# Two-layer adaLN transformer: how the first attention is started up (first head's keys in pieces, its queries placed by matmuls, modulation rows spread over lead chunks)

## The chip, the cores and the metric

One core of one Trainium2 chip. The time is the device time of one execution in microseconds (us). Engines: TensorE (PE; its weight loads PEld), VectorE (DVE), ScalarE (ACT), GpSimd (POOL), and SyncE (SP), which issues the DMAs.

## The reference

Two layers over x of 1024 tokens x 256. Each layer computes six modulation vectors from a condition vector c and then an attention and an expert part:

```
mod = silu(c) @ wmod            -> sa, ca, ga, sb, cb, gb   (256 each)
ga, gb = sign * max(|.|, 0.25)
h = layernorm(x) * (1 + ca) + sa;  x = x + ga * attention(h)
h = layernorm(x) * (1 + cb) + sb;  x = x + gb * experts(h)
```

Attention of layer 0: Q = h @ Wq.T, 16 heads of 16, against 4096 given keys and values per head, softmax, times Wo. Layer 1 has its own projections over the 1024 tokens. The change concerns the start: the modulation vectors of both layers, the first layernorm and projection, and the first head's keys and queries.

## The kernel before, in words

All engines run their own list of instructions; semaphores order them. The order on each engine is written out by hand, so an engine stands still at a wait even where later work is ready.

`Front.register` (lines 966 to 1082) is the start. SP issues the loads in this order: c, x in two halves, the wmod columns of sa and ca of layer 0, the identity, head 0's keys (`load_k`, six loads of 128 KB: three copies into each of two strips of 64 partitions), wq, head 0's values; when the keys have landed, the rest of wmod of layer 0 and all of layer 1. TensorE runs 90 filler matmuls (`keep_busy`, line 1179), the column products of sa and ca (line 1086: one-column matmuls that leave the vector along partitions), 20 fillers, and 16 transposes of the normalised x. ScalarE scales and shifts these into h_t (line 1076).

`Projection` makes Q in four pieces of 128 channels x 512 tokens (line 1282). Each is split into a high part (ScalarE, fp32r, line 1314) and a low part, the rest (VectorE, line 1329), so that a product of parts keeps the precision. Pieces 0 and 1 hold heads 0 to 7. Rows of one head go by DMA (`send_rows`, line 73) into `q_rows`: per strip 48 partitions, high, low, high, against keys high, high, low. GpSimd splits the keys in the same way (`split_keys`: high part of all 128 partitions, line 423; two low parts of 16 partitions, line 428).

`Attention.run` goes over 32 half heads u (512 queries each). First pass, for the row maxima: 16 chunks per half head, each 128 queries x 2 x 512 keys (line 646, two matmuls into one of two bank pairs), reduced by VectorE (line 820). GpSimd splits the maxima in four small steps (line 571 and on), TensorE turns them (line 668), ScalarE puts them beside the queries. Second pass: 32 chunks of scores per half head (line 710), exp by ScalarE (line 912), values (line 689). The first pass runs 22 chunks ahead: 22 lead chunks stand before the first chunk of the second pass.

The later modulation vectors are computed in that lead: two row products (line 1093: c broadcast to 128 columns as weights, 256 columns of wmod moving, so each partition gets the whole row) after 45 fillers before chunk 0, then a group behind each chunk from 2 on, alternately column and row groups, with three fillers ahead of a column group and none ahead of a row; `groups` lists them. All results are taken at once by ScalarE (`take_later`) when the last is there. mod_col holds vectors along partitions, mod_row along the free axis.

The loop that issues the lead chunks:

```
for n in range(ahead):
    first_wait(n)
    if n >= 2: keep_busy(pe, psum, self.ident_bf, filling, 2 * (n % 2))
    first_half(n, 0)
    first_half(n, 1).then_inc(self.s1_full, 1)
    front.later_products(pe, n)
```

## Time and profile before

| | us |
|---|---|
| median of 3 runs | 1781.34 (1774.15 to 1800.0) |
| profiled execution | 1779.75, its span 1777.9 |
| TensorE busy in the span | 1703.0 (96%) |
| VectorE, ScalarE, GpSimd busy | 1388.6, 1149.9, 518.6 |
| mean granted TensorE clock | 0.987 |

Busy time of TensorE counts a matmul that is slow because of a low clock at its slow duration. A row of the timeline merges like instructions that follow each other; x4 is their count. The bracket is the idle time of that engine before it and what ended it. PEclk is the granted clock as a share of full speed.

### The profile page before, as it was taken

What the parts mean: (1) busy time and instruction counts of PE and PEld (TensorE: products, weight loads), DVE (VectorE), ACT (ScalarE), POOL (GpSimd) and SP (SyncE); (2) the same over time, 40 slices, a digit from 0 to 9 for tenths busy, and PEclk for the clock granted to TensorE, in tenths of its full rate; (3) what the DMA queues carried; (4) which work ended last, traced back from release to release, by engine and by line L of the source; (5) the groups of instructions that cost most, each with busy time, mean ns of one, the idle gap of its engine ahead of it and who ended that gap; (6) DMA issues with size and microseconds to landing.
All of it is one profiled execution on the core that took longest, in us unless ns stands there. A gap on an engine that the chain in (4) does not pass through costs nothing. (4 is left out here: it accounts for less than half of the span.)

```text
span 1777.9 us, 33654 instructions
## 1 busy us (share of the span) xinstructions
PE 1703.0 (96%) x12560; PEld 1045.4 (59%) x12563; DVE 1388.6 (78%) x1927; ACT 1149.9 (65%) x2277; POOL 518.6 (29%) x535
## 2 busy tenths in 40 slices
PE   8999999999999999889999989999999999789998
PEld 6433333333333333565444468888888888668886
DVE  4899999999999997367999667677767777746665
ACT  2588888888888888465888545454545454533333
POOL 7446334333344522002334301110211020142221
PEclk8999999999999999989999999999999999989999
DMA  7123322223322300103446210000000000024332
GB/s 177 30 46 65 55 50 45 46 57 75 70 46 57 71 26 11 37 19 57 123 114 165 69 32 16 9 24 15 24 9 24 15 12 0 19 86 115 110 103 77
DMA packets 50305, 97.88 MB, mean 55 GB/s; under 512 B 11481, under 2 KB 21817, under 8 KB 48651
## 3 DMA queue, kind: packets, MB, share of 16 engines
q1 hardware_dynamic: 49899, 95.78, 22.8%
q8 instruction: 78, 1.28, 0.3%
q10 hardware_dynamic: 288, 0.49, 0.2%
q14 instruction: 40, 0.33, 0.1%
HBM read 64.58 MB, written 15.92 MB: 45 GB/s over the span
## 5 line engine op out<-in xcount | busy, mean ns | idle before, releaser
L912 ACT ACTIVATE a_probs<-psum 128x512 f32<-128x512 f32 x1280 | 693.2, 597 | 121.6 <-PE psum L710 91.5
L820 DVE TENSOR_REDUCE a_max_part<-psum 128x1 f32<-128x1024 f32 x512 | 621.8, 1223 | 44.7 <-PE psum L646 42.8
L710 PE MATMUL psum<-a_q_max,a_k_rows 51*128 51x512 f32 x1280 | 409.2, 465 | 0.8 <-ACT a_probs L912 0.7
L689 PE MATMUL psum<-a_probs,a_v_ext 128*32 128x256 f32 (+1 forms) x4600 | 395.1, 415 | 7.3 <-issue 7.2
L646 PE MATMUL psum<-a_k_rows,a_q_rows 48*128 48x512 f32 x1280 | 355.4, 430 | 0.0
L710 PEld LDWEIGHTS psum<-a_q_max,a_k_rows 51*128 51x128 f32 x1280 | 167.0, 184 | 270.1 <-ACT a_probs L912 215.5
L689 PEld LDWEIGHTS psum<-a_probs,a_v_ext 128*32 128x32 f32 x4600 | 91.3, 107 | 206.7 <-issue 105.6
L646 PEld LDWEIGHTS psum<-a_k_rows,a_q_rows 48*128 48x128 f32 x1280 | 152.7, 187 | 9.3 <-issue 3.1
L2228 PE MATMUL psum<-high_t_parts,high_gu 128*128 128x512 f32 x600 | 148.9, 398 | 9.1 <-POOL high_gu L2346 7.5
L816 DVE TENSOR_REDUCE a_neg_max<-psum 128x1 f32<-128x1024 f32 x128 | 150.7, 1219 | 8.2 <-PE psum L646 8.0
L428 POOL TENSOR_TENSOR a_k_rows<-a_k_in,a_k_rows 16x2048 fp32r<-16x2048 f32 x32 | 146.0, 4562 | 2.5
L571 POOL TENSOR_TENSOR a_max_bf<-a_neg_max,a_zeros 128x8 bf16<-128x8 f32 x64 | 14.7, 230 | 443.1 <-issue 392.2
L2228 PEld LDWEIGHTS psum<-high_t_parts,high_gu 128*128 128x128 f32 x600 | 114.0, 191 | 36.6 <-POOL high_gu L2346 8.2
L1792 PE MATMUL psum<-wide_k_t,wide_q_t 128*128 128x512 f32 (+3 forms) x576 | 130.6, 353 | 1.5 <-DVE wide_k_t L1990 1.5
L1792 PE MATMUL psum<-wide_p_t,wide_v 128*128 128x512 f32 (+3 forms) x576 | 109.6, 344 | 5.1 <-DVE x L2001 5.1
L1792 PEld LDWEIGHTS psum<-wide_p_t,wide_v 128*128 128x128 f32 x576 | 97.6, 188 | 22.3 <-issue 6.3
L1933 ACT ACTIVATE wide_probs<-psum,wide_neg_max 128x128 f32<-128x128 f32 (+7 forms) x128 | 96.5, 754 | 21.6 <-DVE wide_neg_max L2023 21.6
L2012 DVE TENSOR_TENSOR wide_p_t<-psum,wide_p_t 128x512 fp32r<-128x512 f32 (+1 forms) x192 | 100.0, 548 | 12.4 <-ACT wide_p_t L1918 12.4
L1792 PE MATMUL psum<-wide_t_parts,wide_wqk 128*128 128x512 f32 x384 | 102.2, 401 | 6.2 <-DVE wide_v L1990 3.9
L1918 ACT ACTIVATE wide_p_t<-psum 128x512 fp32r<-128x512 f32 (+1 forms) x192 | 87.1, 493 | 28.0 <-PE psum L1833 28.0
L1792 PEld LDWEIGHTS psum<-wide_k_t,wide_q_t 128*128 128x128 f32 x576 | 94.0, 188 | 12.6 <-issue 1.9
L2023 DVE TENSOR_REDUCE wide_neg_max<-psum 128x1 f32<-128x128 f32 (+7 forms) x128 | 97.0, 758 | 4.4
(263 smaller groups left out, 2143.2 us busy)
## 6 DMA issues: line engine op xcount, KB each, us to landing
o<-a_o_out SPq DMA_DIRECT2D x56, 256.0 KB, 2.3
a_k_in<-in_k SPq DMA_DIRECT2D x96, 128.0 KB, 4.6
a_q_rows<-q_high SPq DMA_DIRECT2D x124, 64.0 KB, 2.4
gu_in<-in_w_gu SPq DMA_DIRECT2D x25, 256.0 KB, 2.9
high_cw<-cw SPq DMA_DIRECT2D x22, 256.0 KB, 3.9
a_v_in<-in_v SPq DMA_DIRECT2D x16, 256.0 KB, 5.9
a_o<-o SPq DMA_DIRECT2D x8, 512.0 KB, 4.1
wide_qk_in<-in_wqk SPq DMA_DIRECT2D x16, 256.0 KB, 2.8
```

The lines of the kernel that those rows point to most:

```text
L428: pool.tensor_tensor(self.k_rows[low, b, :], self.k_in[low, :], self.k_rows[low, b, :], ALU.subtract).then_inc(self.k_split, 1)
L646: return pe.matmul(psum[:, 2 * (n % 2) + s, :], q_rows[rows, b, q0:q0 + P], k_rows[rows, b, k0:k0 + 512], start=True, stop=True)
L689: mm = pe.matmul(psum[32 * g:32 * g + 32, 7, cols], self.v_ext[:, b, block_at, :], self.probs[:, j % self.pring, cols], start=(j < 4 and f ...
L710: pe.matmul(psum[:, self.bank_of(self.filling(j)), :], k_rows[rows, b, k0:k0 + P], self.q_max[rows, u % 2, :], start=True, stop=True).then ...
L816: dve.tensor_reduce(self.neg_max[:, u % 2, c:c + 1], psum[:, 2 * (n % 2):2 * (n % 2) + 2, :], AX.XY, ALU.max, negate=True).then_inc(self.s ...
L820: dve.tensor_reduce(self.max_part[:, u % 2, c // self.nch, c % self.nch:c % self.nch + 1], psum[:, 2 * (n % 2):2 * (n % 2) + 2, :], AX.XY, ...
L912: act.activation(self.probs[:, p % self.pring, :], psum[:, self.bank_of(self.filling(j)), :], ACT.Exp).then_inc(self.exp_done, 1)
L1792: mm = pe.matmul(out, left(a), right(b), start=(first and n == 0), stop=(last and n == len(PARTS) - 1))
L1933: act.activation(probs[:, i % 2, 0:(i + 1) * P], bank_pair(i)[:, 0:(i + 1) * P], ACT.Exp, bias=neg_max[:, i:i + 1], accum_out=den[:, h % 2 ...
L2012: dve.tensor_tensor(turned_of(i, bank, 1), turned_from(i, bank), turned_of(i, bank, 0), ALU.subtract).then_inc(pt_lo, 1)
L2023: dve.tensor_reduce(neg_max[:, i:i + 1], bank_pair(i)[:, 0:(i + 1) * P], AX.X, ALU.max, negate=True).then_inc(max_ready, 1)
L2228: mm = pe.matmul(psum[:, 2 * (k % 2) + i, :], gu[:, par, a, at:at + P], t_parts[:, b, c, half * 512:(half + 1) * 512], start=(c == 0 and n ...
```

## The change

- Head 0's keys are loaded in four pieces of 512 columns (24 loads of 32 KB) and split piece by piece (`load_first_k`, `split_first_keys`). The first half head goes over its chunks key piece by key piece (`place`).
- Head 0's query rows are no longer sent by DMA. TensorE multiplies the high and low parts with a 0/1 selection matrix (`make_pick`, `pick_queries`), ScalarE copies the result into q_rows.
- The second half of Q: ScalarE also makes a whole copy, and GpSimd subtracts (`low_by_pool`) instead of VectorE.
- The eight later column groups are gone. All ten later vectors are row products, two by two behind lead chunks 3, 4, 6, 7, 10, 11, 13, 14, 16 and 17; other chunks from 2 on have six fillers. The two row products and 45 fillers before chunk 0 go. ScalarE takes each pair as it comes.
- Four of the vectors are needed along partitions: GpSimd multiplies the rows with the identity at u = 2, VectorE sums at u = 4.
- In the front: 120 fillers instead of 90, none behind the column products, ten behind the transposes; wq is issued before the keys; layer 1's wmod waits for layer 0's; VectorE takes the first columns after xn; h_t is half made by VectorE. Where `normalise` of the later layers is concerned, nothing changes; the small tensor `pick` and its memset are there in the second attention too.

```
@@ -405,6 +408,21 @@
+    def place(self, u, c):
+        return (c % 4, c // 4) if u == 0 and self.nch > 1 else (c // self.nch, c % self.nch)
+    def load_first_k(self, sp):
+        for piece in range(self.nch):
+            for n in range(2):
+                part = self.k_dram[0:HD, n * self.per_strip + piece * 512:n * self.per_strip + (piece + 1) * 512]
+                for row in range(STRIP * n, STRIP * n + MROW, HD):
+                    sp.dma_start(self.k_in[row:row + HD, piece * 512:(piece + 1) * 512], part).then_inc(self.k_first[piece], 16)
+    def keys_split(self, eng, h):
+        eng.wait_ge(self.k_split, 2 * (h + self.nch))
     def load_k(self, sp, h):
...
@@ -416,18 +434,38 @@
-    def split_keys(self, pool, h):
+    def split_first_keys(self, pool):
+        for piece in range(self.nch):
+            cols = slice(piece * 512, (piece + 1) * 512)
+            pool.wait_ge(self.k_first[piece], 96)
+            pool.tensor_tensor(self.k_rows[:, 0, cols], self.k_in[:, cols], self.zeros[:, 0:1].broadcast_to([P, 512]),
+                               ALU.add).then_inc(self.k_high, 1)
+            pool.wait_ge(self.k_high, piece + 1)
+            for s in range(2):
+                low = slice(STRIP * s + LOW_K, STRIP * s + MROW)
+                pool.tensor_tensor(self.k_rows[low, 0, cols], self.k_in[low, cols], self.k_rows[low, 0, cols],
+                                   ALU.subtract).then_inc(self.k_split, 1)
+            pool.wait_ge(self.k_split, 2 * (piece + 1))
+    def high_keys(self, pool, h):
+        pool.wait_ge(self.k_loaded, 96 * h)
+        pool.tensor_tensor(self.k_rows[:, h % self.nb, :], self.k_in[:, :], self.zeros[:, 0:1].broadcast_to([P, self.per_strip]),
+                           ALU.add).then_inc(self.k_high, 1)
+    def low_keys(self, pool, h):
         b = h % self.nb
-        pool.wait_ge(self.k_loaded, 96 * (h + 1))
-        pool.tensor_tensor(self.k_rows[:, b, :], self.k_in[:, :], self.zeros[:, 0:1].broadcast_to([P, self.per_strip]),
-                           ALU.add).then_inc(self.k_high, 1)
-        pool.wait_ge(self.k_high, h + 1)
+        pool.wait_ge(self.k_high, h + self.nch)
         for s in range(2):
             low = slice(STRIP * s + LOW_K, STRIP * s + MROW)
             pool.tensor_tensor(self.k_rows[low, b, :], self.k_in[low, :], self.k_rows[low, b, :],
                                ALU.subtract).then_inc(self.k_split, 1)
-        pool.wait_ge(self.k_split, 2 * h + 2)
+        self.keys_split(pool, h)
+    def split_keys(self, pool, h):
+        self.high_keys(pool, h)
+        self.low_keys(pool, h)
...
@@ -459,7 +498,17 @@
         self.clear(pool)
-        self.split_keys(pool, 0)
+        self.split_first_keys(pool)
+    def make_pick(self, dve):
+        dve.wait_ge(self.pick_set, 1)
+        one = self.ident[0:HD, 0:HD].unsqueeze(1)
+        high = self.pick[:, 0, :].rearrange("p (g r) -> p g r", r=32)[:, :, 0:HD]
+        low = self.pick[:, 1, :].rearrange("p (g r) -> p g r", r=STRIP)[:, :, HD:2 * HD]
+        dve.tensor_copy(high, one.broadcast_to([HD, 4, HD])).then_inc(self.pick_ready, 1)
+        dve.tensor_copy(low, one.broadcast_to([HD, 2, HD])).then_inc(self.pick_ready, 1)
...
@@ -582,12 +635,12 @@
             if raw:
+                projection.low_by_pool(pool)
                 self.copy_v(pool, 0)
-                for h in range(1, self.early):
-                    self.split_keys(pool, h)
+                self.high_keys(pool, 1)
                 split_max(0)
-                for h in range(1, self.early):
-                    self.copy_v(pool, h)
+                self.low_keys(pool, 1)
...
@@ -631,16 +686,21 @@
                     pe.wait_ge(self.s1_free, n - 1)
-                if c == 0 and u % 2 == 0:
-                    h = u // 2
-                    pe.wait_ge(self.q_loaded[h % nb], 16 * q_loads * (h // nb + 1))
+                h = u // 2
+                if raw and h == 0:
+                    if c == 0:
+                        pe.wait_ge(self.q_first, u + 1)
+                    if u == 0 and c % 4 == 0:
+                        pe.wait_ge(self.k_split, 2 * (c // 4 + 1))
+                elif c == 0 and u % 2 == 0:
...
@@ -769,10 +829,25 @@
-            projection.products(pe, front)
-            if front is not None:
-                projection.banks_free(pe)
-                front.first_products(pe)
+            def pick_queries(half, bank):
+                cut = slice(half * QH, (half + 1) * QH)
+                pe.wait_ge(projection.low_done, half + 1)
+                if half == 0:
+                    pe.wait_ge(self.pick_ready, 2)
+                for m, part in enumerate((projection.highs[0], projection.lows[0])):
+                    mm = pe.matmul(psum[0:STRIP + MROW, bank, :], self.pick[:, m, 0:STRIP + MROW], part[0:HD, 0, cut],
+                                   start=(m == 0), stop=(m == 1))
+                mm.then_inc(self.q_picked, 1)
+            if front is None:
+                projection.products(pe)
+            else:
+                for n in range(4):
+                    if n == 3:
+                        pick_queries(0, 2)
+                    front.tokens_ready(pe, n % 2)
+                    projection.product(pe, n)
             values_ahead = min(2, projection.tiles)
             for t in range(values_ahead):
...
@@ -786,14 +861,18 @@
+                if front is not None and n == 0:
+                    pick_queries(1, 4)
                 if front is not None:
-                    front.later_products(pe, n)
+                    front.later_products(pe, n, projection, self.q_first)
                 if n == steps + 2:
...
@@ -880,23 +962,31 @@
-            if not raw:
+            def put_first_queries(half, bank):
+                act.wait_ge(self.q_set, 1)
+                act.wait_ge(self.q_picked, half + 1)
+                act.activation(q_rows[0:STRIP + MROW, 0, half * QH:(half + 1) * QH], psum[0:STRIP + MROW, bank, :],
+                               ACT.Copy).then_inc(self.q_first, 1)
+            if raw:
+                projection.high_parts(act, 0)
+                put_first_queries(0, 2)
+                projection.high_and_whole(act)
+                put_first_queries(1, 4)
                 load_table()
...
@@ -925,10 +1015,9 @@
     COL_BANK = 6
+    ROWS = ((3, 0, 2, 5), (4, 0, 5, 5), (6, 0, 3, 7), (7, 0, 4, 7), (10, 1, 0, 6), (11, 1, 1, 6), (13, 1, 2, 4), (14, 1, 5, 4), (16, 1, 3, 7), (17, 1, 4, 7))
...
@@ -975,12 +1064,14 @@
+            sp.dma_start(self.wq, wq_dram).then_inc(self.wq_loaded, 16)
             sp.wait_ge(attention.k_set, 1)
-            attention.load_k(sp, 0)
-            sp.dma_start(self.wq, wq_dram).then_inc(self.wq_loaded, 16)
+            attention.load_first_k(sp)
             attention.load_v(sp, 0)
-            sp.wait_ge(attention.k_loaded, 96)
+            for piece in attention.k_first:
+                sp.wait_ge(piece, 96)
             sp.dma_start(self.wmod[:, 0, :, first:6 * D], by_row[0][:, :, first:6 * D]).then_inc(self.w_loaded[1], 16)
+            sp.wait_ge(self.w_loaded[1], 16)
...
@@ -991,14 +1082,13 @@
+            keep_busy(pe, self.psum, self.ones_bf, 120)
...
             mm.then_inc(self.cols_full, 1)
-            keep_busy(pe, self.psum, self.ones_bf, 20)
...
                                       self.xn[:, t, c * P:(c + 1) * P], self.ident[:, :])
                 mm.then_inc(self.turned_x, 1)
+            pe.wait_ge(self.cols_taken, 2)
+            keep_busy(pe, self.psum, self.ones_bf, 10)
             pe.wait_ge(self.wq_loaded, 16)
-            pe.wait_ge(self.cols_taken, 2)
...
@@ -1040,9 +1131,6 @@
-            dve.wait_ge(self.cols_full, 1)
-            dve.tensor_copy(self.mod_col[:, 0:2], self.psum[:, self.COL_BANK, 0:2]).then_inc(self.cols_taken, 1)
-            dve.tensor_scalar(self.mod_col[:, 2:4], self.psum[:, self.COL_BANK, 2:4], 1.0, None, ALU.add).then_inc(self.cols_taken, 1)
...
@@ -1050,6 +1138,15 @@
             dve.wait_ge(self.id_loaded, 16)
+            attention.make_pick(dve)
+            dve.wait_ge(self.cols_full, 1)
+            dve.tensor_copy(self.mod_col[:, 0:2], self.psum[:, self.COL_BANK, 0:2]).then_inc(self.cols_taken, 1)
+            dve.tensor_scalar(self.mod_col[:, 2:4], self.psum[:, self.COL_BANK, 2:4], 1.0, None, ALU.add).then_inc(self.cols_taken, 1)
+            dve.wait_ge(self.cols_taken, 2)
+            for i in range(2):
+                dve.wait_ge(self.turned_x, 4 * i + 4)
+                dve.tensor_scalar(self.h_t[:, 1, i * 512:(i + 1) * 512], self.psum[:, 2 + i, :], self.mod_col[:, 3:4], self.mod_col[:, 1:2],
+                                  ALU.mult, ALU.add).then_inc(self.h_dve, 1)
...
@@ -1072,79 +1169,83 @@
-                for c in range(DC):
-                    act.activation(self.h_t[:, c, i * 512:(i + 1) * 512], self.psum[:, 2 * c + i, :], ACT.Identity,
-                                   scale=self.mod_col[:, 2 + c:3 + c], bias=self.mod_col[:, c:c + 1]).then_inc(self.h_taken, 1)
+                act.activation(self.h_t[:, 0, i * 512:(i + 1) * 512], self.psum[:, i, :], ACT.Identity,
+                               scale=self.mod_col[:, 2:3], bias=self.mod_col[:, 0:1]).then_inc(self.h_taken, 1)
...
+    def tokens_ready(self, pe, half):
+        pe.wait_ge(self.h_taken, half + 1)
+        pe.wait_ge(self.h_dve, half + 1)
+    def later_products(self, pe, n, projection, q_first):
+        if n not in self.at_chunk:
+            return
+        at = self.at_chunk[n]
+        _, layer, v, bank = self.ROWS[at]
+        if at == 0:
+            pe.wait_ge(self.wide_ready, 2 * DC)
+            pe.wait_ge(projection.low_done, 2)
+        if at == 2:
+            pe.wait_ge(projection.whole_done, 2)
+            pe.wait_ge(projection.high_done, 4)
+        if at == 6:
+            pe.wait_ge(q_first, 2)
+        if at == 8:
+            pe.wait_ge(self.later_taken, 3)
+        pe.wait_ge(self.w_loaded[1 + layer], 16)
         for k in range(DC):
-            mm = pe.matmul(self.psum[:, self.ROW_BANKS[i // 2], (i % 2) * D:(i % 2 + 1) * D], self.c_wide[:, DC * layer + k, :],
+            mm = pe.matmul(self.psum[:, bank, (at % 2) * D:(at % 2 + 1) * D], self.c_wide[:, DC * layer + k, :],
                            self.wmod[:, layer, k, v * D:(v + 1) * D], start=(k == 0), stop=(k == DC - 1))
...
+        return 0 if n in self.at_chunk else 6
...
+        def both(out, n, bank):
+            act.wait_ge(self.later_full, n)
+            act.activation(out.rearrange("p a n -> p (a n)"), self.psum[:, bank, :], ACT.Copy).then_inc(self.later_taken, 1)
+        def apart(first, second, n, bank):
+            act.wait_ge(self.later_full, n)
+            act.activation(first, self.psum[:, bank, 0:D], ACT.Copy).then_inc(self.later_taken, 1)
+            act.activation(second, self.psum[:, bank, D:2 * D], ACT.Identity, bias=1.0).then_inc(self.later_taken, 1)
+        both(self.mod_row[:, 0:2, :], 1, 5)
+        apart(self.mod_flat[:, 0, :], self.mod_flat[:, 1, :], 2, 7)
+        apart(self.mod_flat[:, 2, :], self.mod_flat[:, 3, :], 3, 6)
+        both(self.mod_row[:, 2:4, :], 4, 4)
+        apart(self.mod_row[:, 4, :], self.mod_row[:, 5, :], 5, 7)
+    def keep_diagonals(self, pool):
+        pool.wait_ge(self.later_taken, 8)
+        flat = self.mod_flat[:, :, :].rearrange("p a (c n) -> p (a c) n", n=P)
+        pool.tensor_tensor(flat, flat, self.ident[:, :].unsqueeze(1).broadcast_to([P, 4 * DC, P]), ALU.mult).then_inc(self.diagonals, 1)
+        pool.wait_ge(self.diagonals, 1)
+    def take_columns(self, dve):
+        dve.wait_ge(self.diagonals, 1)
+        dve.tensor_reduce(self.mod_col[:, 4:12], self.mod_flat[:, :, :].rearrange("p a (c n) -> p (a c) n", n=P), AX.X,
+                          ALU.add).then_inc(self.columns, 1)
+        dve.wait_ge(self.columns, 1)
...
@@ -1272,16 +1375,36 @@
+    def high_and_whole(self, act):
+        for half in range(2):
+            n, cut = 2 + half, slice(half * 512, (half + 1) * 512)
+            act.wait_ge(self.full, n + 1)
+            act.activation(self.highs[0][:, 1, cut], self.psum[:, 4 + n, :], ACT.Copy, scale=0.25).then_inc(self.high_done, 1)
+            act.activation(self.whole[:, cut], self.psum[:, 4 + n, :], ACT.Copy, scale=0.25).then_inc(self.whole_done, 1)
+    def low_by_pool(self, pool):
+        for half in range(2):
+            cut = slice(half * 512, (half + 1) * 512)
+            pool.wait_ge(self.high_done, 3 + half)
+            pool.wait_ge(self.whole_done, 1 + half)
+            pool.tensor_tensor(self.lows[0][:, 1, cut], self.whole[:, cut], self.highs[0][:, 1, cut],
+                               ALU.subtract).then_inc(self.pool_low, 1)
+        pool.wait_ge(self.pool_low, 2)
...
```

## Rows read from the trace of the kernel before

**Rows 1.** Stretch, length; busy PE, PEld, DVE, ACT, POOL; PEclk; DMA share; GB/s:

```profile
28.60:34.20 5.60, 4.51 (x34) 2.98 (x33) 5.06 (x5) 0.00 (x0) 0.93 (x1) 1.00 1.05 155
34.20:51.20 17.00, 17.00 (x56) 11.10 (x54) 9.17 (x8) 0.00 (x0) 12.62 (x3) 0.51 0.37 71
51.20:62.00 10.80, 9.38 (x84) 5.71 (x82) 10.03 (x10) 2.50 (x9) 2.17 (x5) 0.99 0.48 74
90.00:400.00 310.00, 306.30 (x2961) 117.33 (x2963) 293.77 (x257) 274.03 (x511) 129.23 (x96) 1.00 0.28 52
```

**Rows 2.** Timeline, front part: start, duration, engine, line, operation, [idle before it]:

```profile
8.95 1.90 PE L1086 MATMUL psum<-a_c_silu,a_o 128*128 128x1 f32 x16
9.41 0.27 POOL L451 MEMSET a_v_ext<- 128x96 f32 x1
11.89 2.14 PE L1009 MATMUL psum<-ident,a_o 128*128 128x128 f32 x16
13.44 2.75 ACT L1076 ACTIVATE h_t<-psum,mod_col 128x512 f32<-128x512 f32 x4
15.21 7.13 PE L1282 MATMUL psum<-h_t,wq 128*128 128x512 f32 x16 [1.18 <-DMA wq<-in_wq]
```

**Rows 3.** Timeline, from projection to the first lead chunk:

```profile
14.55 3.60 POOL L423 TENSOR_TENSOR a_k_rows<-a_k_in,a_zeros 128x2048 fp32r<-128x2048 f32 x1 [4.88 <-DMA a_k_in<-in_k]
18.23 9.10 POOL L428 TENSOR_TENSOR a_k_rows<-a_k_in,a_k_rows 16x2048 fp32r<-16x2048 f32 x2
22.86 1.29 DVE L1329 SCALAR_TENSOR_TENSOR q_low<-psum,q_high 128x512 fp32r<-128x512 f32 x2 [2.58 <-ACT q_high L1314]
24.20 2.69 PE L1179 MATMUL psum<-a_ones_bf 128*128 128x128 bf16 x45 [1.86 <-DVE q_low L1329]
26.73 1.95 PE L1093 MATMUL psum<-a_o,a_c_wide 128*128 128x256 f32 x8
28.60 0.73 PE L646 MATMUL psum<-a_k_rows,a_q_rows 48*128 48x512 f32 x4
29.14 6.88 DVE L820 TENSOR_REDUCE a_max_part<-psum 128x1 f32<-128x1024 f32 x6 [5.00 <-PE psum L646]
```

**Rows 4.** Timeline, lead chunks to the first chunk of the second pass:

```profile
30.42 0.34 PE L1179 MATMUL psum<-ident_bf 128*128 128x128 bf16 x3 [1.09 <-DVE a_max_part L820]
37.56 1.23 DVE L820 TENSOR_REDUCE a_max_part<-psum 128x1 f32<-128x1024 f32 x1 [1.54 <-PE psum L646]
39.22 1.23 DVE L820 TENSOR_REDUCE a_max_part<-psum 128x1 f32<-128x1024 f32 x1 [0.43 <-PE psum L646]
42.27 1.23 DVE L820 TENSOR_REDUCE a_max_part<-psum 128x1 f32<-128x1024 f32 x1 [1.83 <-PE psum L646]
51.66 4.83 DVE L820 TENSOR_REDUCE a_max_part<-psum 128x1 f32<-128x1024 f32 x4 [1.79 <-PE psum L646]
61.41 14.34 DVE L820 TENSOR_REDUCE a_max_part<-psum 128x1 f32<-128x1024 f32 x12
62.10 0.19 PEld L710 LDWEIGHTS psum<-a_q_max,a_k_rows 51*128 51x128 f32 x1
```

**Rows 5.** SP's key loads in the timeline, and transfers of the first 62 us:

```profile
3.29 2.81 SPq L414 DMA_DIRECT2D a_k_in<-in_k  x6
27.36 3.76 SPq L414 DMA_DIRECT2D a_k_in<-in_k  x6
...
a_k_in<-in_k SPq DMA_DIRECT2D x18, 128.0 KB, 5.4
a_o<-in_wmod SPq DMA_DIRECT2D x1, 1536.0 KB, 9.4
```

**Rows 6.** Timeline, steady part: turning the maxima twice, and a 128x1024 product on GpSimd:

```profile
99.33 0.49 PE L668 MATMUL psum<-a_q_rows,a_ident_r 112*115 112x512 f32 x1
119.97 0.49 PE L668 MATMUL psum<-a_q_rows,a_ident_r 112*115 112x512 f32 x1
...
145.85 2.38 POOL L1159 TENSOR_TENSOR gates<-mod_row,a_rec_wide 128x1024 f32<-128x1024 f32 x1
```

149 lines of the change are left out of this document (66 added, 83 removed).

## The prediction

> **What bounds the kernel now.** I read the stretch table first, because the change touches only the start. In the middle of the first attention TensorE is busy 306.30 of 310 us at granted clock 1.00 [rows 1]. There is no work there that an earlier start could take away, and one half head takes 20.64 us (99.33 to 119.97 us) [rows 6]. So whatever is gained is gained before the first chunk of the second pass, at 62.10 us [rows 4], and then everything behind it moves forward as a block. In the same table the stretch 34.2 to 51.2 us stands out: TensorE shows 17.00 of 17.00 us busy, but at clock 0.51, the lower of its two levels (1.2 GHz), and VectorE only 9.17 us busy. In the stretch ahead of it TensorE was busy 4.51 of 5.60 us, in the one behind 9.38 of 10.80 us at 0.99.
>
> The timeline of the first 30 us gives the path to the first lead chunk. Projection starts at 15.21 us, released by the load of wq, and its 16 matmuls take 7.13 us [rows 2]. VectorE's last low part ends at 24.15 (22.86 + 1.29), then TensorE runs 45 filler matmuls (2.69 us) and two row products (1.95 us), and only then the first chunk at 28.60; its reduction starts at 29.14. GpSimd splits the keys of head 0 meanwhile, 14.55 to 27.33 us, so with TensorE free earlier the keys would have held the first chunk [rows 3].
>
> The lead chunks then need 32.96 us (29.14 to 62.10) for 22 chunks. VectorE's reductions set their floor: 1.15 us each (6.88/6) to 1.20 us (14.34/12). Twelve chunks at 1.15 to 1.20 are 13.8 to 14.3 us, and from the reduction of the thirteenth (51.66) to 62.10 the trace shows 10.44 us at the full clock, so 24.2 to 24.7 us would do; I take 24.6. The other 8.4 us are the stretch at the low clock, where two reductions are 3.05 us apart (39.22 to 42.27) with a row product between them [rows 3, 4].
>
> **The change, part by part.** All times are of the profiled execution (span 1777.9 us, 1779.75 us in all), which stands 1.6 us under the median 1781.34.
>
> *Before projection.* Thirty more fillers at 0.06 us (2.69/45) put the column products 1.8 us later; they start 8.95 us now, so 10.75, and end 12.65. The 20 fillers behind them go (1.2 us), so the 16 transposes (2.14 us now, partly waiting for xn) run 12.65 to at latest 14.8. xn is ready earlier, since VectorE no longer waits for the columns before the reciprocal. The four ScalarE evacuations of h_t (2.75 us from 13.44) become two there and two on VectorE, side by side. The first half of h_t is ready near 14.5. wq is issued ahead of the keys and no longer ends the wait. Ten fillers (0.6 us) come last. Projection starts 14.6 to 15.4 instead of 15.21; I take 14.8, a gain of 0.4 [rows 2, 3].
>
> *Queries placed by selection products.* Two pairs of matmuls of 48 or fewer rows by 512 columns; the nearest row, one of 112 x 512, takes 0.49 us, so a pair costs 0.5 (pipelined) to 1.0 us [rows 6]. One pair stands ahead of the fourth projection piece, one behind chunk 0. ScalarE's two copies and the two extra "whole" copies run while TensorE projects. What it removes is the DMA of head 0's queries. Projection plus one pair ends at 14.8 + 7.13 + 0.5 = 22.4 us, and no fillers or row products stand behind it, so the first reduction starts near 23.0 instead of 29.14: **6.1 us gained** [rows 2 to 4].
>
> *Keys in four pieces.* A quarter of 3.60 and of twice 4.55 us is 0.90 and 2.28 us, with gaps 3.3 us a piece. GpSimd ends its memsets at 9.7 us plus one more of about 0.3 us, so pieces could be ready at 13.4, 16.7, 20.0 and 23.4 us, if loaded. Chunks 0 to 3 need only the first, chunk 12 the last. The cover is wide: the last piece is due about 37 us. SP issues 24 loads instead of 6: at 0.47 to 0.63 us each (2.81/6 and 3.76/6) they take 11 to 15 us and end at 15 to 19 us; with the 5.4 us that a key load takes to land, the last piece is there at 20 to 24 us, and split at 24 to 28. The modulation weights queue behind them; the first row product wants them at chunk 3, near 26.5 us. Cost taken: 0; upper bound in the rivals [rows 3, 5].
>
> The table of the Trainium skill, "DMA: Bandwidth & Descriptors", section "Rules for kernel authors", speaks against this: transfers under 64 KB are said to be mostly overhead, and these are 32 KB. Where this would show is the third rival.
>
> *Low parts of the second half and the first value copy on GpSimd.* Two subtractions of 128 x 512 (at most half of the 2.38 us row of 1024 columns and a little, 1.3 us each) stand ahead of head 1's keys, which arrive after 30 us anyway. The subtraction of head 1's low keys, 9.1 us, now stands behind the maxima of the first half head, due near 42 us: ends 53, wanted near 60. Cost 0; if head 1's keys landed after 38 us, their 3.6 us would delay the maxima [rows 3, 5, 6].
>
> *Ten rows in lead chunks.* A row product is 0.97 us at the full clock (1.95/2). With the chunk's two matmuls (0.73 us for the first four, so 0.4 to 0.5) this makes 1.4 to 1.5 us against VectorE's 1.2, two in a row; the spare bank covers most. Between 0 and 0.4 us for each of five pairs: 0 to 2 us, taken 0.5. The eight column groups go, each a string of weight loads with one-column matmuls. With rows or six fillers in every chunk from the third on, TensorE's load is like that of 51.2 to 62 us, where the clock held at 0.99. So I take the low stretch as gone: **8.4 us gained**, less 0.5 [rows 1, 4].
>
> *Columns from rows.* GpSimd: one 128 x 1024 product, 2.4 us, hidden (the two rounds of four small steps for the maxima are a half head apart, and its heaviest work between them, a head's keys and values, is 3.6 + 9.1 + 1.3 us of 20.64). VectorE: one reduction of 128 x 1024, 1.2 us, in the middle of the steady part. VectorE is busy 293.77 of 310 us, so it has 5% to spare, 1.1 us in a half head, but TensorE can wait for a bank at once, so it costs 0 to 1.2; taken 0.8, nearer the full size since TensorE has no time to give back [rows 1, 3, 6].
>
> *Second layer.* One more small memset off the path: 0.
>
> **Sum.** Second pass starts at 23.0 + 24.6 + 0.5 = 48.1 instead of 62.10: 14.0 earlier. Less 0.8: 13.2 us. 1779.75 - 13.2 = 1766.6 us for the profile, 1768.1 on the median.
>
> **Rivals.**
>
> 1. *The clock falls again, for as long as before.* For it: before, it fell with TensorE 80% busy, and chunks 0 and 1 have no fillers. Against: six fillers or a row in all others, and dense projection before. In 17 us at the low clock the pattern row, row, other (3.05 + 3.05 + 1.66, the last from 37.56 to 39.22) passes 6.6 chunks, which cost 7.9 us at the full clock: 9.1 us lost, 1777 us.
>
> The trace shows the clock falling with no wait of TensorE over 1.1 us [rows 4]. The Trainium skill, "TensorE: Matmul & The Clock Gate", section "HAM oscillation", ties such falls to waits for data; by it the fall before, and this rival, would need a longer gap than either kernel has. The trace disagrees for before, so I keep the rival.
>
> 2. *Slower: all ten rows run at the low clock.* A row chunk then takes 3.05 instead of 1.20 us, another 1.66. If the clock falls at chunk 3 and comes back only after 17, this is 10 x 1.85 + 5 x 0.46 = 20.8 us, against a gain of 13.2: 7.6 us slower, 1789 us. It decides from the point where the clock has fallen before chunk 6, so that eight rows (14.8 us and more) lie in it. For it: once low, the clock stayed low for 17 us with TensorE shown fully busy, and rows were among that work. Against: one-column products, gone now, were there too.
>
> 3. *Loads arrive late.* If each key load takes 0.63 us or more to issue and the last lands at 24 us, the weights of layer 0, if they take those 5.4 us too, land at 29.4 and hold chunk 3 for 3 us. Layer 1's, sent only then, land 9.4 us later at 38.8, one us late for chunk 10. Head 1's keys come behind them near 43, and their high part (3.6 us) holds the first maxima for about 1 us. That is 5 us: gain about 8, 1773 us. Against it: now the keys land while 1.6 MB of other loads are ahead of them, and they are there at 14.55 us [rows 3, 5].
>
> **How the numbers follow.** Forecast 0.68, first rival 0.13, slower one 0.06, late loads 0.10, something that gives more than 17 us 0.03. The forecast's own bounds: 6.1 (0.8 less to 0.6 more), 8.4, rows 0 to 2, columns 0 to 1.2 give a gain of 10.5 to 15.5, so 1766 to 1771 on the median. The three timed runs of before lie 26 us apart (1774 to 1800), so the median of a few may be off by 5 to 8 us. With rivals 1 and 3 the range is 1757 to 1779; the slower rival and the tails are left out. About 2% (36 us) is what a measurement of this kernel can tell from no change. No case reaches that: within 0.97, faster 0.02, slower 0.01.
>
> **What would show it.** Projection starts 14.6 to 15.4 us; first reduction 22.5 to 23.5; no stretch below clock 1.00 between 20 and 60 us; reductions of the lead chunks 1.15 to 1.25 us apart; second pass starts at 47.5 to 50; the later half-head period stays 20.64 us, but for one longer by up to 1.2 us. The forecast is wrong if the clock falls in the lead, if chunk 3 waits for the weights, or if the period itself changes.

## The result and the profile after

| | before | after |
|---|---|---|
| median of 20 runs each, us | 1793.01 (1773.22 to 1801.44) | 1769.44 (1765.19 to 1777.86) |
| ratio | | 0.9886, 95% interval 0.9865 to 0.9906 |
| profiled execution, its span | 1779.75, 1777.9 | 1772.17, 1770.3 |
| first reduction of the lead | 29.14 | 23.13 |
| second pass starts | 62.10 | 48.83 |
| mean granted clock | 0.987 | 0.987 |

The change is a gain of 1.1%: by the ratio 20.4 us (0.0114 x 1793), by the medians 23.6 us. The two profiled executions lie only 7.6 us apart. Both numbers need an explanation, for the forecast was 13.2 us.

The front first. This is the timeline of TensorE in the kernel after (start, duration, engine, line, operation, count; in brackets the idle time before it); it answers to [rows 2, 3]:

```profile
1.07 9.42 PE L1280 MATMUL psum<-a_ones_bf 128*128 128x128 bf16 x120 [1.07 <-DVE a_ones_bf L1115]
...
14.71 5.39 PE L1383 MATMUL psum<-h_t,wq 128*128 128x512 f32 x12
20.03 0.48 PE L839 MATMUL psum<-q_high,a_pick 16*112 16x512 f32 x1
20.35 0.39 PE L839 MATMUL psum<-q_low,a_pick 16*112 16x512 f32 x1
20.67 1.98 PE L1383 MATMUL psum<-h_t,wq 128*128 128x512 f32 x4
22.59 0.50 PE L706 MATMUL psum<-a_k_rows,a_q_rows 48*128 48x512 f32 x2
```

Projection starts at 14.71, a pair of picks takes 0.64 us (20.03 to 20.67), and nothing stands between the fourth piece and the first chunk. VectorE then, against [rows 4]:

```profile
23.13 5.75 DVE L900 TENSOR_REDUCE a_max_part<-psum 128x1 f32<-128x1024 f32 x5 [3.40 <-PE psum L706]
29.41 1.22 DVE L900 TENSOR_REDUCE a_max_part<-psum 128x1 f32<-128x1024 f32 x1 [0.52 <-PE psum L706]
...
48.83 0.19 PEld L770 LDWEIGHTS psum<-a_q_max,a_k_rows 51*128 51x128 f32 x1
```

Reductions follow each other with waits of 0.15 to 0.52 us instead of standing 3.05 us apart. The stretch table (busy us of PE, PEld, DVE, ACT, POOL; granted clock; DMA share; GB/s) shows why, and against [rows 1] that the steady part is unchanged; its last row is far behind the change:

```profile
26.00:48.80 22.80, 21.86 (x137) 13.72 (x135) 21.16 (x20) 3.77 (x9) 13.35 (x11) 1.00 0.54 136
90.00:400.00 310.00, 306.29 (x2959) 117.17 (x2951) 294.09 (x256) 273.70 (x511) 135.31 (x99) 1.00 0.26 49
...
1520.00:1545.00 25.00, 22.24 (x141) 20.53 (x142) 16.27 (x52) 13.90 (x35) 3.38 (x5) 0.66 0.11 32
```

The lead has clock 1.00 throughout. The second pass starts 13.3 us earlier, and the first table load of ScalarE behind the attention comes 12.8 us earlier (744.70 to 731.90). At 1526 us, at the head of the last expert part, 11.1 us are left (1537.38 to 1526.26), and then this execution of after lost 3.4 us more, since TensorE's clock fell in the expert part: 22.16 us (1526.26 to 1548.42) for what took 18.78 in the first profile of before. Such falls late in the program show in profiles of both kernels, at different lengths (below), so a single one of them says nothing about the change.

The keys and the loads (GpSimd, and SP's queue, against [rows 3, 5]):

```profile
3.98 11.99 SPq L421 DMA_DIRECT2D a_k_in<-in_k  x24
11.11 1.06 POOL L442 TENSOR_TENSOR a_k_rows<-a_k_in,a_zeros 128x512 fp32r<-128x512 f32 x1 [1.20 <-DMA a_k_in<-in_k]
12.25 2.64 POOL L447 TENSOR_TENSOR a_k_rows<-a_k_in,a_k_rows 16x512 fp32r<-16x512 f32 x2
```

The 24 loads take 12.0 us of SP's queue, 0.50 each. The first piece is split at 14.89, the others start at 14.97, 18.77 and 22.56, the last ends at 26.29.

### The profile page after: what moved, and what is told of

Its sections match the earlier page's. It is cut to its first block and busy times, and to the rows that moved or that the text cites. A ratio compares the mean times of both kernels' runs of the same rounds, so it can differ in the third digit from the quotient of the medians.

```text
span 1770.3 us, 33610 instructions
## 1 busy us (share of the span) xinstructions
PE 1702.0 (96%) x12511; PEld 1045.2 (59%) x12514; DVE 1392.2 (79%) x1930; ACT 1152.1 (65%) x2279; POOL 525.8 (30%) x549
## 3 DMA queue, kind: packets, MB, share of 16 engines
q8 instruction: 78, 1.28, 0.3%
## 5 line engine op out<-in xcount | busy, mean ns | idle before, releaser
L461 POOL TENSOR_TENSOR a_k_rows<-a_k_in,a_k_rows 16x2048 fp32r<-16x2048 f32 x30 | 137.1, 4568 | 2.3
```

The costliest lines, as they stand in the source:

```text
L461: pool.tensor_tensor(self.k_rows[low, b, :], self.k_in[low, :], self.k_rows[low, b, :], ALU.subtract).then_inc(self.k_split, 1)
```

## Experiments

All twelve runs in one table, with the two profiles from above. "Low clock" is where the stretch table in steps of 5 us shows the granted clock well under 1.00 in the first 90 us; "table load" is the first of ScalarE behind 700 us, the end of the part in which every later event only shifts. Ratios are against runs of the kernel before made beside them, not always the same ones, so medians of different rows compare only roughly.

| kernel | us (median, or one run) | ratio (95%) | first reduction | low clock | second pass | table load |
|---|---|---|---|---|---|---|
| before, 1st profile | 1779.75 | | 29.14 | 34 to 51 | 62.10 | 744.70 |
| before_again | 1789.88 | | 29.85 | 11 to 14, 34 to 79 | 67.84 | 754.85 |
| before_third | 1793.15 | | 28.81 | 34 to 75 | 66.20 | 753.12 |
| after, 1st profile | 1772.17 | | 23.13 | none | 48.83 | 731.90 |
| after_again | 1765.61 | | 23.13 | none | 48.84 | 732.59 |
| rows_only | 1774.59 | 0.9899 (0.9850 to 0.9948) | 29.15 | none | 54.70 | 738.45 |
| fill_only | 1777.82 | 0.9939 (0.9911 to 0.9966) | 28.58 | 33 to 40 | 59.20 | 742.53 |
| start_only | 1775.66 | 0.9908 (0.9873 to 0.9944) | 24.15 | 46 to 73 | 51.66 | 743.33 |
| keys_whole | 1776.52 | 0.9923 (0.9895 to 0.9952) | 28.72 | 25 to 38 | 58.06 | 741.07 |
| q_dma | 1781.59 | 0.9944 (0.9918 to 0.9971) | 33.76 | 25 to 41 | 61.88 | 745.64 |
| no_fill | 1779.97 | 0.9936 (0.9907 to 0.9965) | 24.14 | 27 to 50 | 57.52 | 741.72 |
| trimmed | 1771.08 | 0.9887 (0.9842 to 0.9933) | 24.15 | 27 to 33 | 51.91 | 735.21 |
| split_only | 1772.32 | 0.9878 (0.9846 to 0.9911) | 24.16 | 27 to 31 | 51.44 | 734.04 |
| gated | 1768.60 | 0.9884 (0.9855 to 0.9914) | 23.13 | none | 48.82 | 732.15 |

**before_again** and **before_third**: the kernel before, unchanged.

> The kernel before, unchanged, for a second profiled execution. Theory A (the low clock in the lead belongs to its mix of work): a stretch of 15 to 25 us at the low clock between 30 and 55 us again, second pass starts at 60 to 68 us. Theory B (it is a chance of one execution): no such stretch, second pass at 53 to 55 us.

> The kernel before, unchanged, a third profiled execution. Theory A (the low stretch in the lead of before comes in nearly every execution and runs on into the steady part, the first profiled execution was a short one): second pass starts at 64 to 70 us, the clock is at its lower level from about 34 to beyond 60 us, and the run takes 1786 to 1796 us. Rival (the first execution was the usual one and the longer times come from clock falls late in the kernel): second pass at 61.5 to 62.5 us, low stretch of 17 us, and more low clock behind 700 us.

The stretch table of before_again, then of before_third:

```profile
12.00:14.00 2.00, 2.00 (x14) 2.00 (x13) 0.79 (x5) 1.34 (x3) 0.00 (x0) 0.50 1.03 164
...
34.00:52.00 18.00, 18.00 (x62) 11.77 (x60) 10.18 (x9) 0.00 (x0) 12.61 (x3) 0.51 0.43 79
52.00:76.00 24.00, 24.00 (x129) 14.16 (x132) 16.03 (x15) 6.33 (x16) 2.16 (x5) 0.50 0.12 22
```

```profile
34.00:52.00 18.00, 18.00 (x62) 11.87 (x61) 9.87 (x9) 0.00 (x0) 12.60 (x3) 0.51 0.41 75
52.00:76.00 24.00, 24.00 (x135) 13.41 (x138) 16.39 (x16) 7.19 (x18) 2.16 (x5) 0.52 0.10 20
...
1500.00:1600.00 100.00, 85.48 (x473) 72.66 (x472) 58.34 (x132) 45.84 (x100) 22.57 (x19) 0.86 0.12 37
```

Each shows TensorE busy 42 of 42 us in these two windows, at its lower level (1.2 GHz) but for the last 0.7 us of the second profile (the clock is back at 78.9 and 75.3 us): all of the lead that is left from 34 us on, and the first 11 and 9 us of the steady part. The execution on which the forecast stood had 17 us of it and was the short case. before_again reaches the second pass 5.7 us later than that one and the table load 10.15 us later, and its span is 10.2 us longer (1788.1 against 1777.9), so all of the difference arises before the table load. The longer low stretch (34 to 79 instead of 34 to 51 us) is most of it, about 9.4 us. The other 0.7 us were lost before: in this execution alone the clock also fell from about 11 to 14 us (the first row), its 20 fillers there took 2.23 us where the first profile's took 1.28, and the first reduction came 0.71 us later (29.85 against 29.14). before_third has no such early fall, and its half heads are a little longer (20.67 against 20.65 us, see the last section). The last row shows the late falls in before too, by the clock from 1500 to 1600 us: 0.86 there, 0.93 in before_again and 0.95 in the first profile, 0.86 in the first and 0.93 in the second profile of after.

**after_again**: the kernel after, unchanged.

> The changed kernel, unchanged, a second profiled execution. Theory A (six fillers or a row in every chunk keep the clock up): no stretch below clock 1.00 from 20 to 60 us, second pass starts within 0.3 us of 48.83, the run takes 1766 to 1774 us. Rival (the first execution was lucky in the lead, as the one of before was): a low stretch between 25 and 50 us and the second pass 2 to 8 us later.

The lead repeats within 0.01 us, with no low clock. Its span, 1763.8, against the first profile of before, whose expert part took as long (18.78 and 18.79 us between the same two reciprocals), is a gain of 14.1 us, where 13.2 was forecast.

**start_only**: the changed start with the fourteen old groups, column products among them.

```
-        self.at_chunk = {row[0]: i for i, row in enumerate(self.ROWS)}
+        self.groups = [("row", 0, 0), ("row", 1, 0), ("col", 2, 0), ("col", 2, 1), ...
-        return 0 if n in self.at_chunk else 6
+        return 3 if self.groups[at][0] == "col" else 0
```

> The changed kernel with the later modulation vectors computed as before: the 14 old groups (columns and rows alternating, three fillers ahead of a column group) behind lead chunks 3 to 16, no sum over diagonals. First reduction at 23 us in any case. Theory A (the mix of one-column products and few fillers lets the clock fall): low clock within the lead, second pass starts at 55 to 58 us, timed gain over before 5 to 8 us. Theory B (what lets it fall is the gap ahead of chunk 0 that the new start closes): clock stays, second pass at 48 to 49 us, gain as in the whole change, 13 us or more.

**rows_only**: the old start with the ten rows and six fillers elsewhere, no column products.

```
-        self.groups = [("row", 0, 0), ("row", 1, 0), ("col", 2, 0), ...
+    ROWS = ((-1, 0, 2, 5), (-2, 0, 5, 5), (3, 0, 3, 7), (4, 0, 4, 7), ...
```

> The kernel before with only the ten row products (two ahead of chunk 0 as before, the others behind chunks 3, 4, 6, 7, 10, 11, 13, 14; six fillers in the other chunks) and the sum over diagonals. First reduction at 29 us. Theory A: clock 1.00 through the lead, second pass starts at 54 to 56 us, timed gain 7 us or, if most executions of before lose more than the profiled one, up to 14. Theory B: clock falls as before, second pass at 61 us or later, gain about 0.

**fill_only**: the kernel before, with eight fillers ahead of a column group.

```
-        return 3 if self.groups[at][0] == "col" else 0
+        return 8 if self.groups[at][0] == "col" else 0
```

> The kernel before with eight fillers instead of three ahead of each column group, nothing else. Theory A: the added matmuls hold the clock, second pass starts at 54 to 57 us although TensorE has more to do, timed gain 5 us or more. Theory B, and a rival A2 (one-column products are what counts, fillers don't help): clock falls, second pass at 62 to 66 us, no gain or up to 3 us slower.

The stretches of start_only, rows_only and fill_only:

```profile
35.00:45.00 10.00, 10.00 (x68) 7.12 (x66) 9.02 (x9) 0.30 (x5) 4.00 (x3) 1.00 0.30 67
45.00:50.00 5.00, 4.82 (x30) 2.94 (x29) 3.56 (x4) 2.20 (x6) 4.76 (x4) 0.61 0.01 3
50.00:70.00 20.00, 20.00 (x111) 8.59 (x110) 12.75 (x11) 8.79 (x16) 6.06 (x3) 0.50 0.34 52
```

```profile
30.00:55.00 25.00, 22.57 (x150) 13.91 (x150) 23.42 (x22) 3.17 (x8) 14.80 (x8) 1.00 0.59 95
```

```profile
33.00:38.00 5.00, 5.00 (x21) 3.37 (x19) 3.07 (x3) 0.00 (x0) 2.75 (x1) 0.50 0.84 128
38.00:60.00 22.00, 20.57 (x161) 13.85 (x160) 18.07 (x17) 2.65 (x10) 12.05 (x8) 0.96 0.32 66
```

With the rows the lead takes 25.55 us (29.15 to 54.70) and the clock does not fall in it: 7.4 of the 8.4 us of the low stretch are won without any part of the start (32.96 less 25.55; the rest is the 1 us that rows and small waits cost in after too). With the old groups behind the new start it falls at 46 us and stays low into the steady part, so that the table load comes 11.4 us later than in after. More fillers alone leave a fall of about 7 us. Each part alone gives a ratio of 0.99 and both together 0.9886, with intervals that overlap. My reading, which no run separates further, is that rows_only removes the low stretch, the largest term, and start_only has it later and shorter than two of the three profiles of before; it can only be won once.

**keys_whole**: after, but head 0's keys loaded and split as before, in one piece.

```
-        for piece in range(self.nch):
-            pool.wait_ge(self.k_first[piece], 96)
+        pool.wait_ge(self.k_first[0], 96)
```

> The changed kernel with head 0's keys loaded and split as a whole, as before (six loads, one high and two low subtractions); everything else as changed. Theory A (pieces are needed, since GpSimd's 12.7 us for a whole head starts at 12 to 14.6 us): first reduction at 25.5 to 28 us instead of 23.1, second pass 2.5 to 5 us later than the changed kernel's 48.8, timed 3 to 5 us slower than the changed kernel. Rival (TensorE sets the first chunk in any case): no difference.

**q_dma**: after, but head 0's queries by DMA.

```
-                if h > 0 or not raw:
-                    load_q(sp, strips, q_rows[:, h, :], h, self.q_loaded[h])
+                load_q(sp, strips, q_rows[:, h, :], h, self.q_loaded[h])
```

> The changed kernel with head 0's query rows sent by DMA as before, no selection products. Theory A: SP now stands at its wait for layer 0's weights until 23.4 us, then issues layer 1's and only then its three query loads, which take 2 us to issue and 3 to 4 to land: first reduction at 29 to 31 us, that is 6 to 8 us later than the changed kernel, and most of its gain from the earlier start is gone. Rival (the transfer itself is the only cost, 20 to 25 us as before): first reduction at 25 to 26 us, 2 to 3 us later. Either way the clock may fall in the gap that opens ahead of chunk 0.

The first chunk on TensorE in keys_whole, and in q_dma:

```profile
27.89 0.80 PE L703 MATMUL psum<-a_k_rows,a_q_rows 48*128 48x512 f32 x2 [6.62 <-POOL a_k_rows L444]
```

```profile
32.92 1.22 PE L705 MATMUL psum<-a_k_rows,a_q_rows 48*128 48x512 f32 x4 [12.07 <-DMA a_q_rows<-q_high]
```

With whole keys the first chunk waits 6.62 us for GpSimd, with queries by DMA 12.07 us for the query rows, and in both the clock falls near 25 us. So with either part left out the first reduction comes at 28.72 and 33.76 us, and the other part brings almost nothing of the 6 us.

Not all of the 12.07 us is the transfer. In q_dma SP first stands 5.7 us at its wait for layer 0's weights, as the changed order of loads has it, and issues its share of the query rows only at 24.45 us, where ScalarE's share goes out at 18.80:

```profile
24.45 0.63 SPq L73 DMA_DIRECT2D a_q_rows<-q_high  x1
```

Queries by DMA ahead of those weights, which would be the fair rival of the selection products, was not run; q_dma overstates what they are worth. The medians of the two are 7.1 and 12.2 us over that of after; the runs of the kernel before beside them had a median of 1792.28, close to the 1793.01 beside after.

**no_fill** and **trimmed**: after without fillers in the lead; and after with two fillers in the chunk behind a row and six elsewhere, and the diagonals' sum in four reductions.

```
-        return 0 if n in self.at_chunk else 6
+        return 0                                             (no_fill)
+        return 2 if n - 1 in self.at_chunk else 6            (trimmed; 0 in a row's chunk)
```

> The changed kernel without any filler in the lead chunks (ten rows only). Theory A (the share of TensorE's time with streaming matmuls decides): the clock falls in the lead in most executions, second pass at 50 to 60 us in the profile, timed 2 to 12 us slower than the changed kernel. Rival A2 (one-column products were the cause, rows alone are enough): clock stays at 1.00, second pass at 47.5 to 48.8 us, since the fillers behind row pairs go, and timed up to 1 us faster.

> A version that may beat the changed kernel: two fillers instead of six in the chunk behind each pair of rows (the reductions at 29.4 and 38.2 us waited 0.5 us each there), and the sum over diagonals in four parts of 128 x 256 at u = 4 to 7, each within VectorE's slack. Theory: second pass at 47.5 to 48.3 us, the half head at u = 4 back from 21.10 to 20.65 us, 1 to 2 us faster in all if the clock holds. Rival: fewer fillers let the clock fall in some executions, then 5 us or more slower.

**split_only**: trimmed with its six fillers back, so after with four small reductions at u = 4 to 7 alone.

```
-                if u == 4 and front is not None:
-                    front.take_columns(dve)
+                if 4 <= u < 8 and front is not None:
+                    front.take_columns(dve, u - 4)
```

> The changed kernel with the sum over the diagonals of the later columns taken in four reductions of 128x256 at chunks 4 to 7 in place of one of 128x1024 at chunk 4; the fillers stay six. Theory A (the one reduction of 1.2 us cost 0.45 us, since the spare bank takes the rest, and a quarter of it fits into the 5% that VectorE has to spare): the half-head period in which it falls is 20.65 to 20.70 instead of 21.10 us, second pass starts within 0.3 us of 48.83, median 0 to 1 us below the changed kernel's own (ratio 0.986 to 0.989). Rival (the period is lost to another wait at that place): it stays 21.1 us. In the kernel with fewer fillers the clock fell again at 27 us; if it does so here too, the four reductions and not the fillers brought it back.

The same stretches of split_only, trimmed and no_fill:

```profile
27.00:31.00 4.00, 4.00 (x12) 2.42 (x11) 3.00 (x3) 0.00 (x0) 3.66 (x3) 0.57 1.13 295
31.00:35.00 4.00, 3.97 (x27) 2.58 (x25) 3.00 (x3) 0.72 (x2) 0.00 (x0) 1.00 0.97 166
```

```profile
27.00:31.00 4.00, 4.00 (x11) 2.43 (x10) 2.80 (x3) 0.00 (x0) 3.63 (x3) 0.50 1.07 269
31.00:35.00 4.00, 4.00 (x16) 2.16 (x15) 2.28 (x3) 0.60 (x1) 0.00 (x0) 0.68 1.00 159
```

```profile
31.00:35.00 4.00, 4.00 (x11) 2.01 (x9) 2.50 (x3) 0.60 (x1) 0.00 (x0) 0.50 1.03 158
...
45.00:50.00 5.00, 5.00 (x14) 2.53 (x13) 2.90 (x3) 0.66 (x2) 0.00 (x0) 0.50 0.00 0
```

Three kernels with the same start (24.14 to 24.16) lose the clock near 27 us, and what follows goes with the fillers: it is back at 31 us with six, near 33.5 with two behind a row, and only past 50 with none, although TensorE is shown 100% busy there. So the fillers did not keep the clock from falling here; they seem to bring it back. Each of these lengths is one profile, and the same kernel before showed stretches of 17 to 44 us, so the order is an indication. The timed runs agree with it: no_fill has 1779.97 where trimmed, run beside it, has 1771.08, though their intervals overlap.

The late start is not what made the clock fall at 27 us, or not it alone. start_only starts at 24.15 as well, and from 19.66 us up to its first row product its TensorE timeline is that of split_only within 0.02 us. The clock falls during that row product in split_only, and in start_only not before 46 us (start_only first, then split_only):

```profile
26.56 0.50 PE L704 MATMUL psum<-a_k_rows,a_q_rows 48*128 48x512 f32 x2 [0.18 <-DVE a_max_part L898]
26.99 1.13 PE L1199 MATMUL psum<-a_o,a_c_wide 128*128 128x256 f32 x4
```

```profile
26.57 0.51 PE L706 MATMUL psum<-a_k_rows,a_q_rows 48*128 48x512 f32 x2 [0.19 <-DVE a_max_part L900]
27.00 1.58 PE L1208 MATMUL psum<-a_o,a_c_wide 128*128 128x256 f32 x4
```

The four small reductions cost nothing: the half head in which they fall takes 20.65 us, where after has 21.10. But split_only missed its expected second pass by 2.6 us, and its rival is no explanation either, for the first reduction is already 1.0 us late, long before u = 4. Four kernels have that late start (this one, trimmed, no_fill, start_only). VectorE in split_only, against after, shows where it comes from (one line of code: its instructions, the shortest, median and longest duration in ns):

```profile
L1138 DVE TENSOR_SCALAR a_o<-x,a_mv,a_rstd x4: 407/768/1429, 10.2 to 11.9; 128x256 f32<-128x256 f32 x4
```

```profile
L1138 DVE TENSOR_SCALAR a_o<-x,a_mv,a_rstd x4: 406/406/1128, 10.2 to 11.2; 128x256 f32<-128x256 f32 x4
```

The normalisation of x is four equal operations of 406 ns. In after one of them takes 1128 ns, in split_only two are long. GpSimd's first key operation runs from 11.11 to 12.17 in after, from 10.70 to 11.85 in split_only: the keys landed 0.41 us earlier there, and the VectorE operations were caught by it one after the other. A cast of 16x32 behind them takes 1240 ns beside GpSimd's low parts. So an earlier key load makes projection start later, at 15.73 instead of 14.71, with a hole of 0.48 us on TensorE ahead of the ten fillers and one of 0.20 behind them.

**gated**: split_only with one wait; GpSimd starts on the keys once the modulation columns are taken.

```
         self.clear(pool)
+        pool.wait_ge(columns, 2)
         self.split_first_keys(pool)
```

> The kernel with the sum over the diagonals in four reductions, and one wait more: GpSimd starts to split the first piece of head 0's keys only once VectorE has taken the first modulation columns. Theory A (VectorE's four normalisation steps of 128x256, and a cast of 16x32, were held up by GpSimd's key operations that ran beside them: the four took 1.38 us where the keys came later, 2.10 and 3.12 us where they came at 11.0 and 10.7 us): the four steps take 1.38 us again, the columns are taken near 11.8 us instead of 13.6 to 14.6, projection starts near 13.4 instead of 14.7 to 15.7, the first reduction at 21.8 instead of 23.13 or 24.16; no low clock before 60 us; second pass at 47.2 to 48.2 us, if the weights of layer 0 are there for chunk 3 by 24.7 us; median 1.0 to 3.5 us below the kernel with the four reductions alone (ratio 0.986 to 0.987). GpSimd ends head 0's keys near 27.5 instead of 26.3 us, where the last piece is due past 35, so that costs nothing. Rival (the longer normalisation comes from the order of arrival of x or from ScalarE beside it): the four steps stay at 2.1 or 3.1 us and projection starts at 14.7 or later. A third outcome: the start comes 1.3 us earlier, but row products at chunk 3 wait for their weights, TensorE has a gap there, and the clock falls: second pass at 49 to 53 us, no gain.

The normalisation's line, and then timeline rows of GpSimd, TensorE and VectorE:

```profile
L1139 DVE TENSOR_SCALAR a_o<-x,a_mv,a_rstd x4: 400/402/406, 10.2 to 11.2; 128x256 f32<-128x256 f32 x4
```

```profile
12.87 1.04 POOL L442 TENSOR_TENSOR a_k_rows<-a_k_in,a_zeros 128x512 fp32r<-128x512 f32 x1 [2.96 <-DVE mod_col L1145]
...
10.63 1.90 PE L1182 MATMUL psum<-a_c_silu,a_o 128*128 128x1 f32 x16
12.39 1.94 PE L1100 MATMUL psum<-ident,a_o 128*128 128x128 f32 x16
14.17 0.72 PE L1282 MATMUL psum<-a_ones_bf 128*128 128x128 bf16 x10
14.72 5.37 PE L1385 MATMUL psum<-h_t,wq 128*128 128x512 f32 x12
...
11.61 0.16 DVE L512 CAST a_pick<-ident 16x32 fp32r<-16x32 f32 x1
```

All four are 402 ns again and the cast 0.16 us: the contention is shown, by the one wait that removes the overlap. The start is that of after, not the 1.3 us earlier that was expected: this time TensorE is the one that is late, its chain of warm-up matmuls, columns, transposes and ten fillers runs without a hole to 14.72. That chain was late in this execution because its warm-up matmuls got faster only at about 7 us. In keys_whole, where GpSimd's keys also came after VectorE's four operations, they got faster at 4.2 us, the columns began at 9.24 instead of 10.63, and projection at 13.34 (last section). So one profile does not tell what the gate is worth over many executions. The clock stays up, the second pass starts at 48.82, and the six runs lie within 3.3 us (1767.53 to 1770.85), where the six of split_only spread over 8.7 and the twenty of after over 12.7 (with more runs, so a wider spread is to be expected). Its ratio cannot be told from that of after. It is the version I would keep, since VectorE's part of the start no longer depends on when a load lands.

## Why the prediction was right or wrong

**The front, 6.1 us.** Right: 6.0 us (29.14 to 23.13), projection at 14.71 for 14.8, a pair of picks 0.64 within 0.5 to 1.0. One term was missing from the working: VectorE held up by GpSimd at 11 us, worth 0.7 us of normalisation and 1.1 of the cast in after, hidden there, for gated starts projection at the same time without it (its TensorE chain was late), and 1.0 us of the path in four other executions. The Trainium skill, "SBUF — State Buffer", section "SBUF: two separate sides", says that the two engines share a pair of ports, which one of them takes for a whole instruction while the other is fully blocked. The trace agrees: 1.43 us for an operation of 0.41 beside one of 1.15. It was a rule against this change, and I did not weigh it.

**Keys in pieces, loads, third rival.** Right: 3.8 us a piece for 3.3, the last done at 26.29, inside the 24 to 28 given with the loads, and due 37 to 38. The 24 loads cost 0.50 us each, as estimated, and nothing on TensorE's path waited for them; in the lead of after the longest wait of its weight loads for anything is 0.8 us, and of its matmuls 0.4. The rule of the Trainium skill, "DMA: Bandwidth & Descriptors", section "Rules for kernel authors", that transfers under 64 KB are mostly overhead, fits SP's time (12.0 us for 24 loads, 2.8 for the six of before with the same bytes) and decides nothing here.

**The lead, 24.6 + 0.5.** Right: 25.70 us (23.13 to 48.83) for 25.1; rows and other small waits cost 1.1 where 0.5 was taken, inside 0 to 2. rows_only gives 25.55 with the old start.

**The columns, 0.8.** 0.45 us (21.10 less 20.65), inside 0 to 1.2, and 0 when cut in four.

**The sum, 13.2.** For the pair of executions that it was made for, the second pass came 13.3 us earlier where the steps gave 14.0, and the first part of the program ended 12.8 us earlier. The upper bound of the gain was added up wrongly: 6.7 + 8.4 with nothing off is 15.1, not 15.5, and nothing rests on it. The 2% below which I expected to tell nothing was too cautious: with twenty runs of each kernel the interval, 0.9865 to 0.9906, leaves out 1.

**What was mis-sized is the price of the low clock before, 8.4 us.** I took it from one execution, in which the low stretch ended inside the lead. In the two others it runs on to 79 and 75 us, and they reach the table load 10.2 and 8.4 us later, of which about 9.4 and 8 go with the longer stretch. The three profiles of before reach that at 750.9 us on average, the two of after at 732.2: 18.6 us, which is most of the 20.4 to 23.6 timed. The rest may lie in the late falls of the clock, which these profiles show to differ between executions; that is not settled. The starting point was off in the same way: the median of three runs, 1781.34, lay 11.7 us under that of twenty. A base that was too fast and a gain that was too small cancelled: that 1768.1 came within 1.3 us of 1769.44 is luck. Measured as a gain, the result is what I had given a chance of 0.03 (more than 17 us). The spread of the three runs, 26 us, was in the text; I read it as noise about the median, where three different profiles now suggest different lengths of one stretch.

**First and second rival.** The clock did not fall in the lead in either profile of after, nor in gated. But it did near 27 us in three of the four kernels with the late start, and it came back after about 4 us with all fillers, and after 24 us with none. The condition of the second rival, ten rows at the low clock, arose in no_fill, which has its first eight rows in a low stretch: its lead took 33.4 us (24.14 to 57.52), 7.7 us more than that of after, not the 20.8 that I had worked out, and the kernel stayed faster than before. A row took 2.07 us there and row chunks stood 2.73 us apart (27.28 to 30.01), where 3.05 was taken; the rest of the difference was not taken apart, and no_fill has no fillers that would be slow too. The rule of the Trainium skill, "TensorE: Matmul & The Clock Gate", section "HAM oscillation", that such falls come with waits for data, holds for a part: keys_whole and q_dma have waits of 6.6 and 12.1 us, and there the clock fell at 25 us; in before it fell with none over 1.1 us. Both kinds of fall exist in this kernel. What makes the clock fall at 27 us in three kernels, no run here shows. It is not the late start with its holes of 0.7 us or more at 14 to 16 us by itself, for start_only has the same start, 1.35 us of holes (0.41, 0.74 and 0.20), and clock 1.00 up to 46 us. Nor do the four profiles without a fall in the lead (after, after_again, gated, rows_only) show that it never comes there.

## What to carry to other kernels

When the clock is low in a stretch of one profile, look at two more profiles before pricing it: the stretch can end by chance, and its length is then the largest number in the sum. In such a stretch, replacing one-column matmuls by wide ones, or putting cheap fillers between matmuls, can be worth more than its own time: in the profiles here the clock then stayed up or came back sooner (rows_only, fill_only, split_only), though why is not shown. When an operation is moved ahead on GpSimd, list what VectorE does in those microseconds, and if it is on the path, gate GpSimd behind it.

## What was unexpected of the hardware

- The granted clock stayed at 1.2 GHz for 44 and 41 us with TensorE shown busy in every one of them (before_again, before_third), through the lead and 11 and 9 us into the steady part, whose work holds 2.4 GHz from 90 us on.
- Four VectorE operations of 0.41 us took 1.38, 2.10 or 3.13 us as GpSimd's key operation began after them, at 11.1 or at 10.7 us; a landing 0.4 us earlier cost 1.0 us.
- The half-head period is 20.647 us in some executions and 20.672 in others, throughout the execution and for the same kernel (after 20.65, after_again 20.67): 0.8 us over thirty half heads, whatever the kernel.
- The clock's record begins only some microseconds into the program, and the views print 1.00 where it has no entry. In after its first entry is at about 6.4 us, and the warm-up matmuls of 128x128 get faster just there: 31 of them fall into the 3 us from 2 to 5, and 58 into the 3 us from 7 to 10 (a window also counts the ones that it cuts, so the rows below show 12 and then 22 in one microsecond). So the 1.00 in the first row is no measurement. The moment differs between executions, from 3.9 us (q_dma) to 7.1 us (gated), and with it the start of the column products behind them: 9.09 us in q_dma, 9.24 in keys_whole, 10.63 in gated. The start of the kernel moves by up to 1.5 us before any data matter. The stretch table of after:

```profile
5.00:6.00 1.00, 1.00 (x12) 1.00 (x11) 0.45 (x2) 0.31 (x2) 1.00 (x2) 1.00 1.07 367
6.00:7.00 1.00, 1.00 (x17) 1.00 (x15) 0.96 (x3) 0.00 (x0) 1.00 (x3) 1.00 1.08 405
7.00:8.00 1.00, 1.00 (x22) 1.00 (x20) 0.96 (x3) 0.00 (x0) 1.00 (x1) 1.00 1.06 373
```
